# Heads in the two halves of the partitions, norms centred by VectorE, and a new order of turns, in a six-layer transformer

## The reference

```python
for i in range(6):
    xn = adaln(x, noise_emb, n1_w[i], n1_b[i])           # layer norm, then scale and shift
    q, k, v = split(xn @ qkv_w[i].T)                     # 16 heads x 8
    x = x + attn(rope(q), rope(k), v, src_mask) @ so_w[i].T      # 512 queries, 512 keys
    xn = adaln(x, noise_emb, n2_w[i], n2_b[i])
    q, k, v = rope(xn @ cq_w[i].T), rope(context @ ck_w[i].T), context @ cv_w[i].T
    x = x + attn(q, k, v, ctx_mask) @ co_w[i].T                  # 512 queries, 77 keys
    xn = adaln(x, noise_emb, n3_w[i], n3_b[i])
    x = x + gelu(xn @ f1_w[i].T + f1_b[i]) @ f2_w[i].T + f2_b[i]
# attn: softmax(q k / sqrt(8) + mask) v
```

## Time and profile before

| | |
|---|---|
| median of 3 runs | 4610.91 us (4610.57 to 4612.44) |
| profiled execution: time, span | 4613.32 us, 4611.5 us |
| TensorE busy | 4031.0 us, 87% |
| VectorE busy | 3249.7 us, 70% |
| ScalarE busy | 2277.7 us, 49% |
| GpSimd busy | 407.0 us, 9% |
| mean granted clock of TensorE | 0.91 |

### The profile page before, as it was taken

The page is one execution under the profiler, slowest core; times in us unless marked ns, Lnnn a source line. Parts: engine busy times, 40 slices in busy tenths (PEclk is TensorE's granted clock), DMA queues, the critical chain, the costliest instruction groups (busy, mean ns, idle before and its releaser), DMA issues. The chain is left out here.

```text
span 4611.5 us, 83547 instructions
## 1 busy us (share of the span) xinstructions
PE 4031.0 (87%) x24597; PEld 2622.9 (57%) x24597; DVE 3249.7 (70%) x16939; ACT 2277.7 (49%) x7483; POOL 407.0 (9%) x338
## 2 busy tenths in 40 slices
PE   8999999999999999876888888888887346979897
PEld 6888888888888888653333333333333223644456
DVE  7888888888888888665666666666664455456543
ACT  5555555555555555432655555555555222236432
POOL 0000000000000000011111111111111010024310
PEclk9999999999999999886988888888888667989998
DMA  0000000000000000012122222222220002500001
GB/s 30 2 2 2 2 2 2 2 2 2 2 2 2 2 2 2 15 43 69 27 50 54 50 54 50 54 50 54 49 51 17 5 4 72 139 30 6 11 10 42
DMA packets 92091, 121.98 MB, mean 26 GB/s; under 512 B 28292, under 2 KB 75583, under 8 KB 91396
## 3 DMA queue, kind: packets, MB, share of 16 engines
q1 hardware_dynamic: 91651, 116.82, 10.0%
HBM read 85.42 MB, written 30.53 MB: 25 GB/s over the span
## 5 line engine op out<-in xcount | busy, mean ns | idle before, releaser
L297 DVE CUSTOM_DVE_ANT_0 I-197junk<-I-193encw,I-196expo,I-205rec 128x77 f32<-128x77 f32 x3072 | 945.6, 356 | 7.0
L1335 DVE TENSOR_REDUCE I-41263nmax<-ps 128x1 f32<-128x512 f32 x768 | 500.9, 686 | 201.8 <-PE ps L1003 192.0
L1223 ACT ACTIVATE I-41266prob<-ps 128x512 f32<-128x512 f32 x768 | 428.4, 595 | 238.1 <-PE ps L1040 235.5
L275 ACT ACTIVATE I-195tanh_s<-ps 128x77 f32<-128x77 f32 x1024 | 241.3, 236 | 594.9 <-PE ps L255 594.9
L255 PEld LDWEIGHTS ps<-I-190hist,I-49small 128*128 128x128 f32 x2048 | 304.6, 188 | 298.3 <-DVE I-190hist L333 298.3
L255 PE MATMUL ps<-I-190hist,I-49small 128*128 128x77 f32 x2048 | 456.4, 304 | 0.2
L261 PE MATMUL ps<-I-195tanh_s,I-49small 128*128 128x77 f32 x2048 | 454.6, 304 | 0.0
L262 PE MATMUL ps<-I-190hist,I-49small 128*128 128x128 f32 x2048 | 439.5, 296 | 0.0
L257 PE MATMUL ps<-I-190hist,I-194uh_h 128*128 128x128 f32 x2048 | 439.5, 296 | 0.0
L283 ACT ACTIVATE I-201hh<-I-207gate_t,I-206pre,I-200rh 128x1 f32<-128x1 f32 x1024 | 395.5, 386 | 88.0 <-DVE I-206pre L297 0.2
L1003 PE MATMUL ps<-I-41257kS,I-41256qS 96*128 96x512 bf16 x768 | 346.2, 470 | 83.0 <-DVE I-41263nmax L1335 58.0
(11 more groups left out here) (542 smaller groups left out, 7062.9 us busy)
## 6 DMA issues: line engine op xcount, KB each, us to landing
I-41256qS<-parts SPq DMA_DIRECT2D x96, 192.0 KB, 4.9
parts<-I-41275room SPq DMA_DIRECT2D x36, 384.0 KB, 2.5
parts<-I-41275room SPq DMA_DIRECT2D x36, 256.0 KB, 2.1
I-41257kS<-parts SPq DMA_DIRECT2D x48, 192.0 KB, 4.6
I-61029spread<-gates_rows SPq DMA_DIRECT2D x24, 256.0 KB, 4.1
I-61030spread<-gates_rows SPq DMA_DIRECT2D x22, 256.0 KB, 4.1
I-61031spread<-gates_rows SPq DMA_DIRECT2D x22, 256.0 KB, 4.0
parts<-I-41275room SPq DMA_DIRECT2D x36, 128.0 KB, 1.8
```

Of the source, the lines that this page charges most:

```text
L297: return e.tensor_tensor_reduce(junk[:, 2 * g + b, :], encw[:, g, b, :], expo[:, b, :], inv[:, b:b + 1], rec[:, b, g:g + 1], ALU.mult, ALU ...
L1223: e.activation(prob[:, tau % 2, j, :], k.ps[:, b, :], ACT.Exp, scale=scale).then_inc(free[b], 1)
L1335: e.tensor_reduce(nmax[:, U % HG, i, j:j + 1], k.ps[:, use[0], :], AX.X, ALU.max, negate=True).then_inc(free[use[0]], 1)
```

## The change

1. **Layout.** `qS`, `kS` and `cS` have half as many columns. Head h stands in partitions 64 x (h mod 2) and up: 48 rows of parts, the mask in row 48, the maxima in rows 49 and 50. A matmul takes 49 rows (maxima) or 51 (scores). Every `spread` and every mask transfer becomes two, one for each half; the bytes are the same. The waits count 32 where they counted 16.
2. **Fills.** `kS` and `cS` are filled with ones once. Before they were filled with zeros, and then two rows of each with ones.
3. **Cross maxima.** The four matmuls that share one PSUM bank now belong to heads of one half (two heads, two blocks of queries), and the next bank has those of the other half. Before they were four heads of one block. The reduction writes through a strided view.
4. **Norms.** `find_shift` and the `shift` tile are gone. VectorE makes `xh` itself, (z - mean) x root, in four instructions.
5. **Order.** All five order strings are new. Some of their shape, as counts: in one layer TensorE's string still has 436 turns, VectorE's 226, SyncE's 52 and GpSimd's 32; ScalarE's has 232 where it had 238. In TensorE's, the 18 + 6 turns of m that followed the cross values are now 15 + 2, and the cross maxima stand together with no turn of a between them.

```diff
-ROWS_QK = 96
-ROW_MAX = 96
-ROWS_ALL = 128
+ROWS_QK = 49
+ROW_MAX = 49
+ROWS_ALL = 51
...
-        qS = sbuf(ctx, nc, "qS", [ROWS_ALL, B, NH, T], BF16)
-        kS = sbuf(ctx, nc, "kS", [ROWS_ALL, B, NH, T], BF16)
-        cS = sbuf(ctx, nc, "cS", [ROWS_ALL, B, NH, S], BF16)
+        qS = sbuf(ctx, nc, "qS", [P, B, NH // 2, T], BF16)
+        kS = sbuf(ctx, nc, "kS", [P, B, NH // 2, T], BF16)
+        cS = sbuf(ctx, nc, "cS", [P, B, NH // 2, S], BF16)
...
                     for dst, at, m in ((kS, c * T, T), (cS, B * T + c * S, S)):
-                        e.dma_start(dst[ROW_MASK:ROW_MASK + 1, c, :, :],
-                                    maskrow[:, at:at + m].unsqueeze(1).to_broadcast([1, NH, m])).then_inc(s.sent, 16)
+                        for u in range(2):
+                            e.dma_start(dst[64 * u + ROW_MASK:64 * u + ROW_MASK + 1, c, :, :],
+                                        maskrow[:, at:at + m].unsqueeze(1).to_broadcast([1, NH // 2, m])).then_inc(s.sent, 16)
...
-                e.memset(kS[:].rearrange("p c h t -> p (c h t)").bitcast(F32), 0.0).then_inc(s.filled, 1)
-                e.memset(cS[:], 0.0).then_inc(s.filled, 1)
-                e.wait_ge(s.filled, 2)
                 for dst in (kS, cS):
-                    e.memset(dst[ROW_MAX:ROW_MAX + 2], 1.0).then_inc(s.filled, 1)
+                    e.memset(dst[:], 1.0).then_inc(s.filled, 1)
...
+            def head(tile, c, h, rows):
+                return tile[64 * (h % 2):64 * (h % 2) + rows, c, h // 2, :]
...
-                            e.matmul(k.ps[:, b, :], qS[0:ROWS_QK, c, 4 * m + j, i * P:(i + 1) * P],
-                                     kS[0:ROWS_QK, c, 4 * m + j, :], start=True, stop=True,
+                            e.matmul(k.ps[:, b, :], head(qS, c, 4 * m + j, ROWS_QK)[:, i * P:(i + 1) * P],
+                                     head(kS, c, 4 * m + j, ROWS_QK), start=True, stop=True,
...
-                                for j in range(4):
-                                    mm = e.matmul(k.ps[:, b, j * S:(j + 1) * S],
-                                                  qS[0:ROWS_QK, c, 4 * g + j, i * P:(i + 1) * P],
-                                                  cS[0:ROWS_QK, c, 4 * g + j, :], start=(j == 0), stop=True,
-                                                  skip_group_check=True)
+                                for n in range(4):
+                                    y, q = divmod(n, 2)
+                                    x, h = 2 * (i // 2) + y, 4 * g + 2 * q + i % 2
+                                    mm = e.matmul(k.ps[:, b, n * S:(n + 1) * S], head(qS, c, h, ROWS_QK)[:, x * P:(x + 1) * P],
+                                                  head(cS, c, h, ROWS_QK), start=(n == 0), stop=True, skip_group_check=True)
...
-                    def find_shift(name):
+                    def centre(name):
                         e.wait_ge(s.rstd, norm[r, name] + 1)
-                        e.scalar_tensor_tensor(shift[:, half], k.mv[:, half, 0], -1.0, k.rstd[:, half], ALU.mult,
-                                               ALU.mult).then_inc(s.shifted, 1)
+                        for i in range(TPB * c, TPB * (c + 1)):
+                            e.tensor_scalar(k.xh[:, i, :], z[:, i, :], k.mv[:, i, 0:1], k.rstd[:, i:i + 1], ALU.subtract,
+                                            ALU.mult).then_inc(s.norm, 1)
...
-                        n = NH // len(jsent[name])
+                        n = NH // 2 // len(jsent[name])
                         for g, landed in enumerate(jsent[name]):
-                            e.dma_start(dst[0:ROW_MASK, c, n * g:n * g + n, :], src[:, n * g:n * g + n, :]).then_inc(landed, 16)
+                            for u in range(2):
+                                e.dma_start(dst[64 * u:64 * u + ROW_MASK, c, n * g:n * g + n, :],
+                                            src[:, 2 * n * g + u:2 * n * g + 2 * n:2, :]).then_inc(landed, 16)
```

More of the change, by code:

```diff
@@ L755 @@
-    sync=("rrrrrrrrrrmrmrrrrrmrrmmrrrrrrrrrrmrrrrmmrrrrrrrrrrrrrrrmrrrrrrrmm",
-        "mrrrrrrrrrrrrrrrmrrrrrrrmmmrrrrrrrrrrrrrrrmrrrrrrrmm",
+    gpsimd=("rrrrrrrrrraaarrrrrrrrrrarrraarrrrrrrrrrarrraa",
+        "rrrrrrrrrrarrraarrrrrrrrrrarrraa",
+        3,
+        "rrrrrrrrrrarrraarrrrrrrrrrarrraarrrrrarrraarrrrrrrr"),
+    vector=("rrrrrrrmmmmmmmmmmmmmmmmmmmrmmmmmmmmmmmmmmmmmrmmmmmmmmmmmmmmmmmrmmmmmmmmmmmmmrmmraaamammmmamarmrrmmmrmrmrmmmmmm"
+            "mmmmmmmrrrrrrrrrrrrrrrrrrrrmmmmmmmmmmmmrrrrrmmrmrmmmmmmmmmmmmmmrmmrmmmmmmmmrmmmmraaararaarrrmmmrmrmrmmmmmmmmmm"
+            "mmmmrrrrrrrrrrrrrrrrrrrrmmmmmmmmmmmmmmmmmrrrmrrmmrmrmmmmmmmmmmmmmmmrmmmrmmmmmmrmmmmrrraaaaaar",
+        "rrmmmrmrmrmmmmmmmmmmmmmmrrrrrrrrrrrrrrrrrrrrmmmmmmmmmmmmmmmmmrrrmrrmmrmrmmmmmmmmmmmmmmmmmrmrmmmmmmrmmmmrrraaaa"
+        "aarrrmmmrmrmrmmmmmmmmmmmmmmrrrrrrrrrrrrrrrrrrrrmmmmmmmmmmmmmmmmmrrrmrrmmrmrmmmmmmmmmmmmmrmmmmmrmmmmmmrmmmmrraa"
+        "araaar",
+        3,
+        "rrmmmrmrmrmmmmmmmmmmmmmmrrrrrrrrrrrrrrrrrrrrmmmmmmmmmmmmmmmmmmrrrrrmmrmrmmmmmmmmmmmmmmrmmrmmmmmmmmrmmmmraaarar"
+        "aarrrmmmrmrmrmmmmmmmmmmmmmmrrrrrrrrrrrrrrrrrrrrmmmmmmmmmmmmmmmmmrrrmrrmmrmrmmmmmmmmmmmmmrmmmmmrmmmmmmrmmmmraaa"
+        "raraarrrmmmmmmmrmmmmmmmrmmmmmrmmmmmmmmmmmrmrmrrmrmrmrmrrmrrmrmrmrrmrmrmrrmrmmmmmmmmmmmmmmmmmmmmmmmmrrrrrrraaaa"
+        "ararrrrrrrrrrrrrrrrrrrrrrrrrrrrrrrrrr"),
@@ L815, in transformer @@
         identb = sbuf(ctx, nc, "identb", [P, P], BF16)
-        shift = sbuf(ctx, nc, "shift", [P, NT])
         nmax = sbuf(ctx, nc, "nmax", [P, HG, TPB, 4])
@@ L1039, in attend @@
                                 e.wait_ge(free[b], 2 * tau + j // 2)
-                            e.matmul(k.ps[:, b, :], kS[0:ROWS_ALL, c, 4 * n + j, x * P:(x + 1) * P],
-                                     qS[0:ROWS_ALL, c, 4 * n + j, :], start=True, stop=True,
+                            e.matmul(k.ps[:, b, :], head(kS, c, 4 * n + j, ROWS_ALL)[:, x * P:(x + 1) * P],
+                                     head(qS, c, 4 * n + j, ROWS_ALL), start=True, stop=True,
                                      skip_group_check=True).then_inc(full[b], 1)
@@ L1127, in rest @@
                                 b = open_bank(e, use)
-                                e.matmul(k.ps[0:S, b, :], cS[0:ROWS_ALL, c, 4 * g + j, :],
-                                         qS[0:ROWS_ALL, c, 4 * g + j, :], start=True, stop=True,
+                                e.matmul(k.ps[0:S, b, :], head(cS, c, 4 * g + j, ROWS_ALL),
+                                         head(qS, c, 4 * g + j, ROWS_ALL), start=True, stop=True,
                                          skip_group_check=True).then_inc(full[b], 1)
@@ L1233, in rest @@
                     mine = nT[:, c * T:(c + 1) * T]
-                    def centre(name):
-                        e.wait_ge(s.shifted, norm[r, name] + 1)
-                        for i in range(TPB * c, TPB * (c + 1)):
-                            e.activation(k.xh[:, i, :], z[:, i, :], ACT.Identity, scale=k.rstd[:, i:i + 1],
-                                         bias=shift[:, i:i + 1]).then_inc(s.norm, 1)
                     def keep_norm(name, layer, n):
@@ L1263, in rest @@
                     if r >= B:
-                        centre("ln2")
-                        yield
                         keep_norm("ln2", l, 1)
@@ L1430, in rest @@
                         yield
-                        find_shift("ln2")
+                        centre("ln2")
                         yield
@@ L1445, in rest @@
                                 e.wait_ge(*made(use))
-                                e.tensor_reduce(cmax[:, g, i, :], k.ps[:, use[0], 0:4 * S].rearrange("p (j n) -> p j n", j=4), AX.X,
+                                e.tensor_reduce(cmax[:, g, 2 * (i // 2):2 * (i // 2) + 2, i % 2:4:2],
+                                                k.ps[:, use[0], 0:4 * S].rearrange("p (y q n) -> p y q n", y=2, q=2), AX.X,
                                                 ALU.max, negate=True).then_inc(free[use[0]], 1)
```

104 lines of the change are left out of this document (45 added, 59 removed).

## The result

The changed kernel takes **4798.7 us** (median of four runs, 4794.5 to 4802.3) against 4611.7 of before: ratio 1.0405, 95% interval 1.0387 to 1.0423. I had predicted 4536 us and a range up to 4625. It is slower by 187 us, by more than rival A gave (4673 us).

What follows compares the result with a forecast made beforehand. VectorE and the clock were taken to bound each round's first half, TensorE's order and streaming its second. Terms summed to -5.2 us a round, x 11 = -57, plus -17.5 at the start: 4536 us, range 4460 to 4625.

Steps and rivals of the forecast that it cites:

- rival A: Second half of each round: half-high matmuls fail to keep the clock up, 25 us more low clock, 4673 us; chance 0.18.
- the clock: Start of each round's second half: TensorE begins at low clock for 6.6 us, costing +3.3 us (0 to 8).
- the signs that I named for a wrong prediction: Round over 120 us, second half's clock below 0.9, or gap at a change of shape near 0.2 us.
- The re-cut: First half of a round, cross values to first cross score: shortened from 36.6 to 24.6 us, -12.0.
- Moved work: Second half of each round: 20 matmuls and 3 weighings moved there from the first half, +7.4 us.
- Overlap and switches: Each round: opposite-half pairs running together, -7.4 us; 42 more shape changes at 0.10 us, +4.2 us.
- rival B: Second half of each round: banks free singly, so pairs never start together; +7.4 us a round, 4617 us; chance 0.14.
- Centring: Norms in each round: VectorE's form replaces ScalarE's, one exposed norm gets shorter, -0.7 us.
- The start: Before the modulation matmuls: fewer fills let SyncE send the mask earlier, -17.5 us once (bounds -16 and -18.1).

Runs made afterwards that it cites:

- short_49: Kernel before with attention maxima cut to 49 partitions and scores to 51, all heads in the lower partitions, simpler fills: 4904.9 us.
- short_49_new_order: Kernel before's layout cut to 49 and 51 partitions, no pairing of heads, with the changed kernel's order and VectorE centring: 5018.3 us.
- full_height: Changed kernel with every attention product on all 128 partitions, so no overlap, and output not the reference's: 4639.6 us.
- old_layout_new_order: Kernel before's layout and product heights (96 and 128 partitions) with the changed kernel's order and VectorE centring: 4670.9 us.
- norms_only: Kernel before with VectorE centring alone, everything else in its old order: 4594.5 us.
- start_norms: Kernel before, old order and heights, with VectorE centring and a shorter start through simpler fills: 4574.8 us.
- layout_only: Kernel before, with its own order and norms, given the changed kernel's layout of paired heads: 4706.0 us.
- halves_64: Changed kernel with maxima padded from 49 to 62 partitions and scores from 51 to 64: 4723.0 us.

## Why the prediction was wrong

**The step that failed is the clock**: "between 0 and 16 us of it, I take 6.6: +3.3". The second half has 43.5 us more of low clock than before. Of these 19.9 stand at its start (20.1 us against 0.2), where I had looked and put a bound of 16; the other 23.6 stand further in (31.7 us against 8.1), where I had put nothing. At 0.45 us each (an estimate between 0.48 from short_49 against before and 28.7 us for 66.7 = 0.43 from short_49_new_order against full_height) that is +19.6. What my step had wrong is that a busy TensorE brings the clock back soon: on products of 49 and 51 partitions it does not (33.25 us busy at 0.50 in short_49). With whole-array products in the order of after the clock is up 1.3 us into the second half on average (full_height), with those of after 20.1 us. I bounded the term by how late the clock rises after the first half, and left the height of the products to rival A at 0.18. The main ground against A was the earlier trace rows: that two heads of 64 rows last as long as the whole-array row behind them. That row shows one product at full clock, among other work; it cannot show what a whole stretch of short products does to a low clock. The clock round it is 1.00 from 4110 to 4330 in before, and a high clock is just what short products leave alone. The ground for A stood in the earlier trace rows, TensorE busy for 9.4 of 10 us at the low level, and I gave it too little weight. A was the right mechanism, though not by letting the clock fall but by not bringing it back, and its own size (25 us beside my 6.6) was too small. Two of the signs that I named for a wrong prediction came true: a round takes 137 us (I said 120), and the second half has a clock of 0.76 (I said 0.9).

**The re-cut** of the first half: I took -12.0, measured -7.5. The baseline of 36.6 us was one round; the mean is 35.4. The 24.6 were nearly met in every second round (25.4), the others take 27.1. In the nine middle rounds the saving is 9.7 us; the first round (27.6 and 27.3) saves nothing and the eleventh, the first of the last layer, is longer (39.6 and 45.4). I had given all eleven the pace of one.

**Moved work**: I took +7.4. old_layout_new_order against norms_only has 13.5 us more in the second half, less 4.0 us of low clock at 0.45: +11.7. The 44 instructions that moved are the ones that I had priced (8 maxima, 12 scores, 3 weighings of 8 instructions each), so the other 4.3 us are not forgotten products. TensorE's idle time in the second half is 13.3 us on average against 10.2: 3.1 us of waits that the new order makes and my sum put at nothing. The last 1.2 us I cannot place.

**Overlap and switches**: I took -7.4 (34 x 0.22 is 7.5) and +4.2, together -3.2. Together they come out at -3.8 by the estimate above (-3.1 to -4.4); no run separates the two, and that the sum agrees so closely is in part luck. The counts behind them do hold: in the nine middle second halves of after 33 to 40 neighbouring pairs start less than 0.1 us apart (I took 34 of 46), which answers rival B, and the gap at a change is 0.1 us. So little was won there that nothing was left to pay for the clock.

**Centring**: -0.7 taken, -1.9 measured with all that follows from it (norms_only). **The start**: -17.5 taken, -18.1 measured; start_norms against norms_only, -19.6.

The terms as they come out, those with low clock in them estimates at 0.45: -7.5 + 11.7 - 3.8 - 0.9 (the centring in the second half, 1.7 less its own low clock) + 19.6 = +19.1 a round, where the rounds differ by 17.6. By whole kernels: the layout costs 93 us (layout_only), in which height is +289 and pairing with its shorter start -196; the centring gives 21; the order costs 115 on this layout (the rest up to 187), 101 on halves_64, 76 on the old one. The order was not neutral even apart from the clock, and no rival of mine said so.

What stays open: why products of fewer partitions do not bring the clock back when the engine is as busy, what share the added changes of shape have in it, and what holds the clock down in the first half at full height.

## What to carry to other kernels

Before cutting matmuls to fewer partitions, price the clock and not only the streaming time: a product with zeros in its spare rows can cost the same 0.22 us, as here, and let the engine come back to 2.4 GHz. Test it by padding alone, since a change of a few rows leaves every instruction and wait in place. And test an order written for one layout on the other: here layout, order and centring had three prices of different sign, and only the centring and the start were worth keeping.

## What was unexpected of the hardware

- Two stretches of 25 us in the same order, TensorE busy for 23.8 and 23.9 us: clock 0.67 with products of 49 and 51 partitions, 1.00 with 128.
- In short_49 TensorE is busy for all of 33.25 us and the clock stays at 0.50; then it stays at 1.00 for 37.5 us on the same kinds of products. Height shows in how long the clock stays low, not in whether it can stay high.
- Rows that hold nothing but zeros times ones count: before and short_49 compute the same values with the same instructions, fills apart, and differ by 289 us.
- Two short products in opposite halves at the same time leave less low clock than the same products one after the other: 51.8 us in the second half against 77.7.
- From 96 to 126 partitions of the maxima, with the scores at 128, little or nothing changed (4574.8 and 4571.8 us).
